# Four tables of due times that order the last stage of a transformer kernel

## The reference

```python
def attn_layer(x, Wqkv, qs, ksc, Wo):
    q, k, v = jnp.split(x @ Wqkv, 3, -1)          # 16 heads of 64
    q = l2norm(q) * qs
    k = l2norm(k) * ksc
    q = q * cos * scale + rotate_half(q) * sin * scale
    k = k * cos * inv + rotate_half(k) * sin * inv
    out = local_attention(q, k, v)                # windows of 32, look one window back
    return out.reshape(b, n, INNER) @ Wo
def ffn_layer(x, g, bln, W1, b1, W2, b2):
    xn = (x - mu) / jnp.sqrt(var + 1e-05) * g + bln
    a, gate = jnp.split(xn @ W1 + b1, 2, -1)
    return a * jax.nn.gelu(gate, approximate=False) @ W2 + b2
for i in range(6):
    x = attn_layer(shift_tokens(x), ...) + x
    x = ffn_layer(shift_tokens(x), ...) + x
```

## Time and profile before

| | |
|---|---|
| median of 3 runs | 4813.31 us |
| the profiled execution | 4813.55 us, its span 4812.2 us |
| PE, DVE, ACT, POOL busy in the whole span | 87%, 83%, 67%, 78% |
| the same from 2500 to 3000 us, within the six layers | 95%, 91%, 70%, 91% |
| granted TensorE clock there | 0.98 of full |
| six-layer stage | from 1403.6 us to the end |

### The profile page before, as it was taken

How to read it: one execution, slowest core, us unless ns; L and a number is a source line. 1 busy time by engine, 2 the same in 40 slices (tenths; PEclk the granted TensorE clock), 3 DMA queues, 4 the chain that set the end, 5 groups by cost and what they waited for, 6 DMA issues and landing times.

```text
span 4812.2 us, 139104 instructions
## 1 busy us (share of the span) xinstructions
PE 4202.0 (87%) x57664; PEld 3071.6 (64%) x57664; DVE 3984.8 (83%) x6471; ACT 3222.5 (67%) x5034; POOL 3739.2 (78%) x2624
## 2 busy tenths in 40 slices
PE   7886566558867999999999999999999999999997
PEld 5664455446645676666676666666666667766666
DVE  4665989945558899898998899988998899988994
ACT  4664888845435677676776677776776677766775
POOL 1112888834359999899998999989998899989994
PEclk9998778879989999999999999999999999999999
DMA  2000000000001222222222222222222222222222
GB/s 61 2 2 1 1 1 1 1 26 2 2 1 35 52 54 62 58 54 55 51 62 59 57 52 52 64 56 57 52 61 53 57 52 53 63 58 56 54 53 59
DMA packets 120832, 198.72 MB, mean 41 GB/s; under 512 B 66896, under 2 KB 78224, under 8 KB 120080
## 3 DMA queue, kind: packets, MB, share of 16 engines
q1 hardware_dynamic: 120208, 189.82, 16.0%
HBM read 24.12 MB, written 2.10 MB: 5 GB/s over the span
## 4 chain that ended last, share of the span: by engine, by line
PE 48%; DVE 16%; ACT 11%; issue 9%; DMA 8%; POOL 6%; SPq 2%; DVEq 0%; ACTq 0%; POOLq 0%
PE ps L1306 9%; DMA arena<-arena 7%; PE ps L1250 7%; PE ps L1251 6%; DVE arena L1489 3%; PE ps L1259 3%; ACT arena L1376 2%; PE ps L1317 2%; DVE arena L1482 2%; DVE arena L1481 2%; DVE arena L598 2%; PE ps L1347 2%; PE ps L1358 2%; DVE arena L1505 2%; PE ps L344 2%
## 5 line engine op out<-in xcount | busy, mean ns | idle before, releaser
L1577 POOL TENSOR_TENSOR arena<-arena 128x32 f32<-128x32 f32 x192 | 1046.0, 5448 | 183.9 <-DVE arena L1491 183.9
L1582 POOL TENSOR_TENSOR arena<-arena 128x1024 f32<-128x1024 f32 x384 | 930.9, 2424 | 23.9 <-DVE arena L1482 23.9
L1481 DVE TENSOR_TENSOR arena<-ps,arena 128x1024 f32<-128x1024 f32 x384 | 468.6, 1220 | 203.8 <-ACT arena L1376 189.7
L1306 PE MATMUL ps<-arena 96*64 96x64 f32 x12288 | 437.9, 232 | 167.3 <-DMA arena<-arena 111.3
L1376 ACT ACTIVATE arena<-ps 128x1024 f32<-128x1024 f32 x384 | 393.0, 1023 | 281.9 <-PE ps L1251 276.1
L1399 ACT ACTIVATE arena<-ps 96x1024 f32<-96x1024 f32 x384 | 390.6, 1019 | 277.7 <-PE ps L1290 277.7
L208 POOL TENSOR_SCALAR arena<-arena 128x2 f32<-128x2 f32 x256 | 73.4, 287 | 635.7 <-DVE arena L202 624.7
L1306 PEld LDWEIGHTS ps<-arena 96*64 96x64 f32 x12288 | 412.8, 145 | 220.7 <-issue 216.4
L1600 POOL TENSOR_TENSOR arena<-arena 128x1536 f32<-128x1536 f32 x192 | 529.0, 2755 | 14.6 <-DVE arena L1515 14.6
L1482 DVE TENSOR_TENSOR arena<-ps,arena 128x1024 f32<-128x1024 f32 x384 | 466.2, 1214 | 0.0
L1250 PE MATMUL ps<-arena 128*128 128x512 f32 x768 | 442.0, 659 | 6.0 <-DVE arena L1507 5.0
(11 more groups left out here) (251 smaller groups left out, 10134.0 us busy)
## 6 DMA issues: line engine op xcount, KB each, us to landing
arena<-arena SPq DMA_DIRECT2D x192, 384.0 KB, 4.3
arena<-arena SPq DMA_DIRECT2D x192, 256.0 KB, 3.7
arena<-arena SPq DMA_DIRECT2D x192, 128.0 KB, 2.3
arena<-in_dWqkv SPq DMA_DIRECT2D x18, 512.0 KB, 3.7
arena<-arena SPq DMA_DIRECT2D x96, 64.0 KB
arena<-arena SPq DMA_DIRECT2D x96, 63.5 KB
arena<-in_dWo SPq DMA_DIRECT2D x6, 512.0 KB, 5.3
arena<-in_x SPq DMA_DIRECT2D x4, 512.0 KB, 7.3
```

Of the source, the lines that this page charges most:

```text
L1306: i = pe.matmul(p[64 * (h % 2):64 * (h % 2) + 64, 128 * (h // 2) + 64 * blk:128 * (h // 2) + 64 * blk + 64], v[:, blk, 64 * h:64 * h + 64] ...
L1481: dve.tensor_tensor(o1, p.rearrange("p (h e) -> p h e", h=16), bc(cs, 1, 16), ALU.mult)
L1577: pool.tensor_tensor(ss[:, 0:32], ss[:, 32:64], mhalf32, ALU.pow).then_inc(*S.rs.up())
L1582: pool.tensor_tensor(a1[:, half], a1[:, half], T2[:, half], ALU.add).then_inc(*radd[g].up())
```

## The change

The four tables get other numbers and nothing else is touched: the same instructions, buffers and semaphores.

```diff
-    TILE = {"ro0": 654, "ro1": 705, "q0": 1004, "radd0": 1103, "q1": 1110, "rs": 1112, "ssum": 1216, "sq0": 1412,
+    TILE = {"radd0": 0, "radd1": 114, "rs": 635, "ro0": 924, "ro1": 1055, "ssum": 1085, "halo": 1229, "nrm0": 1313,
...
-    LAYER = {"tab": 16000, "lqk": 32160, "lv": 37208, "lwo": 38282, "lw1": 46228, "lw2": 46350}
-    EDGE = {"e0": 18150, "e1": 19210, "e2": 21160, "e3": 21210, "out": 23580}
+    LAYER = {"lqk": 32650, "lv": 37700, "lwo": 38900, "lw1": 47700, "lw2": 48200, "tab": 16000}
+    EDGE = {"e0": 19570, "e1": 20630, "e2": 22580, "e3": 22630, "out": 25000}
```

More of the change, by code:

```diff
@@ L1203, in phase_d @@
     FB = [(stats(C), sb([128, 2]), sb([128, 2, 128]), sb([128, 2, 128]), sb([128, 3, 256])) for _ in range(NF)]
-    TILE = {"ro0": 654, "ro1": 705, "q0": 1004, "radd0": 1103, "q1": 1110, "rs": 1112, "ssum": 1216, "sq0": 1412,
[4 rows of a table removed]
-    BATCH = {"sh": 0, "xs": 592, "fd": 11434, "fst": 11472, "frs": 12694, "fn": 14770, "ft": 15147, "fgm": 15848,
-             "fzT": 15882, "fg": 15993, "fge": 16105, "fa": 16128, "fo": 16150, "xxf": 16220}
-    LAYER = {"tab": 16000, "lqk": 32160, "lv": 37208, "lwo": 38282, "lw1": 46228, "lw2": 46350}
-    EDGE = {"e0": 18150, "e1": 19210, "e2": 21160, "e3": 21210, "out": 23580}
+    TILE = {"radd0": 0, "radd1": 114, "rs": 635, "ro0": 924, "ro1": 1055, "ssum": 1085, "halo": 1229, "nrm0": 1313,
[4 rows of a table added]
+    BATCH = {"sh": 189, "xs": 558, "fd": 10497, "fst": 12624, "frs": 13777, "fn": 16105, "ft": 16779, "fgm": 16933,
+             "fg": 16960, "fzT": 17348, "fge": 17533, "fa": 17592, "xxf": 17640, "fo": 17970}
+    LAYER = {"lqk": 32650, "lv": 37700, "lwo": 38900, "lw1": 47700, "lw2": 48200, "tab": 16000}
+    EDGE = {"e0": 19570, "e1": 20630, "e2": 22580, "e3": 22630, "out": 25000}
     order = [(1000 * (NT * l + k) + t, piece, l, k) for piece, t in TILE.items() for l in range(depth) for k in range(NT)]
```

## The result

The changed kernel took 4881.78 us in the median of four runs (4875.0 to 4890.0), beside 4813.43 for the kernel before: ratio 1.0144, 95% interval 1.0124 to 1.0166. It is slower, as forecast (4840, range to 4890), but by 68 us and not by 27. The profiled execution took 4875.73 us for a span of 4874.4, 62.2 more than before. What follows accounts for these 62; the other 6 lie within the spread of the changed kernel's own executions.

What follows compares the result with a forecast made beforehand. PE was taken to set the pace, at 33.68 us a pair. Pairs of 34.25 us gave +49 us over 86 pairs, changes of layer -27 and the ends +5: +27, 4840 us, range 4780 to 4890.

Steps and rivals of the forecast that it cites:

- `o` to `v`: PE from o to the next v, with t0 moved in: 8.97 us in the odd half, 10.2 in the other.
- `v` to `o`, odd tile: PE waits 1.2 us at fo for ACT's pT0, so o starts 7.8 us after v; bounds of the wait 0 and 2.
- `v` to `o`, even tile: PE's fg waits for the slot that DVE's xxa frees: 7.0 us, plus 0.2 of port wait, 7.2.
- the sum of the pair: Two tiles on PE: 8.97 + 7.2 + 10.2 + 7.8 = 34.2, with late copies 34.25 us against 33.68; +49 us over 86 pairs.
- I take nothing for it: Ramp up: POOL's new order lets k's rotary go earlier; priced at nothing, with -5 us left in the range.
- no instruction is added or removed, so PE's 32.5 stay: PE's own work stays about 32.5 us a pair, the floor in either order.
- about 0.1 for copies that land late: Allowance of about 0.1 us a pair for copies of v landing later than the median 4.3 us, 5.4 at most.
- Changes of layer: Weight loads on SP's queue: one long wait of o goes, one shortens, one lengthens; -5.5 us each, five times, -27.
- A: Rival: no wait at PE's fo, the copy of v rules both halves; 4765 us, put at 4785; chance 22 in 100.
- B: Rival: the pair gets 0.2 to 0.3 us longer and the changes of layer pay for it; 4813 us; chance 15 in 100.
- C: Rival: each ssum on DVE waits 2 us for POOL's add, +2.4 a pair; 5040 us, or 4940; chance 6 in 100.
- D: Rival: POOL's rs holds up DVE's nrm1 by 2.1 us twice a pair, 1.2 coming through; 4940 us; chance 2 in 100.

Runs made afterwards that it cites:

- the last experiment: Kernel before, with the four weight loads each behind a vd and POOL's frs behind rs: 4686.76 us, ratio 0.9733; without the frs move 4740.33.

## Why the prediction was right in direction and too small

**`o` to `v`: right in the odd half.** In the pair shown it is 3063.29 - 3054.32 = 8.97, as predicted; the other half, 10.34 for 10.2, comes below.

**`v` to `o`, odd tile: right.** From the last v matmul (3045.36 + 1.02 = 3046.38) to `o` it is 7.94, predicted 7.8; the wait for ACT 1.02, predicted 1.2. The wait is shorter than predicted and `o` still later, since PE comes to `fo` after 4.1 us and not after 3.8. That the chain costs what it seems to cost is shown by `fn` moved: 33 us alone, 90 - 29 = 61 with the copy covered.

**`v` to `o`, even tile: right.** `fg` waits 0.49 for `xxa`, as said. 7.2 was predicted, and over the layers the median is 7.21. The pair shown has 3070.83 - 3063.29 = 7.54, of it 0.27 of wait for a late copy, which the next part counts.

**The step that failed is the sum of the pair, 34.25 for 34.81, and with it "I take nothing for it" in the ramp up.** The pair missed by 0.56 us in two terms of about the same size.

The first is "no instruction is added or removed, so PE's 32.5 stay". The quietest pairs of the changed kernel, those without a late copy, take 34.44 us (half pairs of 16.90 and 17.54), where my terms summed to 34.17. Less the waits of 1.02 and 0.49 that is 32.9 us of PE's own work; the same instructions took 33.60 - 1.13 = 32.5 before. A piece costs up to some 0.1 us more or less with the piece ahead of it, and I priced each by its old neighbours. Two lines of the old order:

```profile
3021.62 1.02 PE L1250 MATMUL ps<-arena 128*128 128x512 f32 x2
...
3028.99 1.95 PE L1317 MATMUL ps<-arena 128*128 128x128 f32 x16
```

In the new order, above, `q0` behind `t0` takes 1.13, and `wo` behind a transpose 2.05. So `o` to `v` of the other half takes 10.34 and not 10.2, and `v` to `o` of the odd tile 7.94 and not 7.8: 0.27 a pair, 23 us over 86 pairs.

The second is "about 0.1 for copies that land late". I took the landing's median (4.3 us) as the bound and its tail (up to 5.4 in the stretch I read) as rounding. Over the layers it lands 3.9 to 6.4 us after its issue, and before it was 4.0 to 6.3. The pair lies 0.37 above its quietest, of which I had 0.1: another 0.27, 23 us. 0.27 of the 0.37 stand in the two stretches as waits of `o` for the copy (4.6 and 0.7 us in 19.5 pairs); the last 0.1 no row accounts for.

Late copies belong to the sum, but they are not what made the changed kernel slower than the one before. It waits less for the copy: 35.4 us from 1900 to 4550 us, where it was 79.7, and without the long waits at the changes of layer 19.2, where it was 25.7. The old pair of 33.68 had such waits in it. What grew is `o` to `v`, from 18.2 to 19.4 us a pair in the two stretches: `t0` moved in twice. `v` to `o` gave up that work and yet stayed at 15.5, where I had it fall to 15.0: the slots of `p0` and `wo`, PE's neighbours and the copy took it all back.

The third is the ramp, priced at nothing and worth 12.8 in this trace. It waits 20.3 us for the copy from 1520 to 1690 us, where it was 14.0. How much of the 12.8 comes from that is not settled: `t0` put back took 16.6 us of these waits away, and its ramp was still 292.1 us long, against 284.3 in the kernel before.

**Changes of layer: right in sign, half the size.** -54 instead of -27. `lw2`: `o` waited 3.6 to 4.5 us behind it before and at most 0.7 after. I took 5 to 6 for wait and slow stretch; by the 3 us that the slow stretch costs when `lw2` is put back, 7 is my estimate. `lv` was to keep a long wait, "shortened by some 1 to 2 us"; it was 3.6 to 4.4 us and is at most 0.6. The order there differs in `fd`, which no longer stands between `lv` and `vd`, but no run separates that. `lwo` kept its wait, 2.4 to 3.9 us where it was 2.5 to 3.2. That error of -27 hid some of the error above, which is luck.

**End: +8.1 for +5.** One more batch runs alone; the size was close.

From the forecast's +27 to the trace's +62: PE's own work +23, tail +23, ramp +13, end +3, less 27 of the layers; the rest is what lies ahead of the stage and rounding.

**Rivals.** A (no wait at `fo`) was wrong in every pair. B (it comes out even) is 68 us off. C and D did not happen: 503 ns in the median and 515 at most for 1491, 1217 at most for `nrm1`. In C, 2.0 and 0.6 make 2.6 and not 2.4. D also started from a wrong reading: `nrm1` stood beside `rs` in the kernel before as well, in all 35 cases from 2400 to 3000 us. For `nrm1` the rule of the Trainium skill (SBUF — State Buffer, Who interferes with whom) again does not show, though `rs` is under way beside it for 5.4 us; whether because the power's instruction reads little from SBUF, no run here tells. The other way round something shows: in 18 of these cases before, POOL's add started 0.8 us into `nrm1`, and it took some 2.64 us instead of 2.37, the longest of this line:

```profile
L1582 POOL TENSOR_TENSOR arena<-arena x70: 2352/2368/2647, 2400.4 to 2996.5; 128x1024 f32<-128x1024 f32 x70
```

In the changed kernel no add starts beside `nrm1`, and the longest takes 2.38. For 1491 and POOL's add the rule does show, and the last experiment made 53 us out of it.

What stays open: the share of `fd` in the changes of layer, most of the ramp's loss, and what makes a copy land late.

## What to carry to other kernels

Ask of a piece that moves what latency it covered, and whether the stretch that it leaves can get shorter at all: here it could not, in either half. Price a latency by its tail, not its median, and a piece by its new neighbours. Moving one piece on the engine that claims PSUM slots in turn can change who waits for whom in every slot (`fa`, and `t0` in the kernel before). Moves on the other engines leave the slots as they are, but they are not safe for that: `fn`, `frs` and the loads gained, while the exponent (+117), `xxa` (+67) and `fd` with `lw2` (+639) lost, each by making something behind it late. A weight load ahead of a transfer on the critical path costs the time until its own release, so put it right behind.

## What was not expected of the hardware

The landing of the copy's third DMA (384 KB, inside the chip) varies from 3.9 to 6.4 us, in the halves without `fd` too. The long ones go along with packets of the queue that loads instructions (462 of 16 KB in the whole span, below, from the page of the changed kernel). Of the 173 copies of the layers the 31 that met no such packet landed within 4.43 us, and all 47 that took over 5 us had met one; but so had 95 others that did not. This is seen together in the trace and was not tested.

```profile
q8 instruction: 462, 7.57, 0.7%
```

A tensor_scalar of 182 ns on DVE can wait out most of a POOL add of 2.4 us (2141 ns). In the changed kernel it starts 0.2 to 0.3 us before the add's end in all 35 cases, and what it then takes depends on POOL's next instruction: with the copy of `halo` behind the add it is done 0.04 us after the add's end, in some 0.27 us in all; with the memset of `halo` (0.32 us) it waits that out too and takes 0.51.

An idle PE costs more than its idle time: behind the waits of 6.55 us in the mean that `lw2` put back caused, each place lost some 3 us more, with 0.50 of the clock granted at the one shown.
